# Pooling and projection of an audio layer as one stage, with the row evictions shared between engines

## The reference

```
scores  = sum over features of x * w + b          # per time step
weights = softmax over each window of 8 steps
h       = sum over the window of x * weights      # 94 tokens of 64 features
y       = layernorm(h)
q, k, v = y @ w_qkv.T + b_qkv                     # 8 heads of 8
qgr,kgr = qr(q).Q, qr(k).Q                        # per batch and head
a       = softmax(conv(bn([q.k * s, (q.k)^2 * s, (qgr.kgr)^2 * s])))
h       = h + (a @ v) @ w_proj.T + b_proj
h       = h + ffn(layernorm(h))                   # 16 routed experts and a shared one, 2 layers
```

## Time and profile before

| | |
|---|---|
| median of 3 runs | 902.47 us (901.5 to 903.48) |
| the profiled execution | 902.73 us, its span 900.8 us |
| PE busy | 763.8 us (85%), 16453 instructions |
| PE weight loads busy | 562.5 us (62%) |
| DVE busy | 709.7 us (79%), 1333 instructions |
| ACT busy | 440.2 us (49%), 949 instructions |
| POOL busy | 492.7 us (55%), 532 instructions |
| mean granted TensorE clock | 0.917 |

### The profile page before, as it was taken

How to read it: one execution, slowest core, us unless ns; L and a number is a source line. 1 busy time by engine, 2 the same in 40 slices (tenths; PEclk the granted TensorE clock), 3 DMA queues, 4 the chain that set the end, 5 groups by cost and what they waited for, 6 DMA issues and landing times. The chain is left out here.

```text
span 900.8 us, 38915 instructions
## 1 busy us (share of the span) xinstructions
PE 763.8 (85%) x16453; PEld 562.5 (62%) x16453; DVE 709.7 (79%) x1333; ACT 440.2 (49%) x949; POOL 492.7 (55%) x532
## 2 busy tenths in 40 slices
PE   3577857888616699999999999999999998799994
PEld 2233324666514578777788777788777776366663
DVE  4388895666699489998999998999998998376772
ACT  2234332444302166655556555556655555277773
POOL 3255572000000578888888888888888884122220
PEclk9688886999858599999999999999999999599998
DMA  8766300222410122222222222222222220001111
GB/s 288 279 209 233 107 1 11 43 44 44 105 49 1 60 63 64 62 65 77 65 63 62 64 63 71 71 63 62 62 65 77 66 63 23 1 19 30 30 27 33
DMA packets 65450, 64.99 MB, mean 72 GB/s; under 512 B 39001, under 2 KB 55964, under 8 KB 65308
## 3 DMA queue, kind: packets, MB, share of 16 engines
q1 hardware_dynamic: 64780, 61.24, 22.3%
q10 hardware_dynamic: 528, 1.54, 0.5%
HBM read 52.93 MB, written 6.75 MB: 66 GB/s over the span
## 5 line engine op out<-in xcount | busy, mean ns | idle before, releaser
L1113 ACT ACTIVATE sq<-ps_dot 128x376 f32<-128x376 f32 x384 | 165.0, 482 | 145.7 <-PE ps_dot L1010 145.7
L1010 PE MATMUL ps_dot<-q_st,k_blk 64*64 64x94 f32 x6144 | 170.5, 249 | 1.0 <-ACT sq L1113 0.8
L1010 PEld LDWEIGHTS ps_dot<-q_st,k_blk 64*64 64x64 f32 x6144 | 134.6, 134 | 47.3 <-issue 28.8
L943 POOL TENSOR_TENSOR v_blk<-v_rep,vmask 128x384 f32<-128x384 f32 x128 | 106.7, 855 | 10.6 <-PE ps_m L1040 6.3
L958 POOL TENSOR_TENSOR half<-prob 128x564 f32<-128x564 f32 x64 | 75.6, 1181 | 60.6 <-ACT prob L1108 60.6
L965 POOL TENSOR_TENSOR k_blk<-k_cm,hmask 128x768 f32<-128x768 f32 x64 | 96.7, 1511 | 1.8 <-PE ps_a L1052 1.8
L967 POOL TENSOR_TENSOR k_mix<-k_cm,cols 128x768 f32<-128x768 f32 x64 | 96.8, 1512 | 0.0
L1136 DVE TENSOR_REDUCE row_max<-ps_a 128x94 f32<-128x564 f32 x128 | 88.9, 736 | 5.2 <-PE ps_a L1060 5.2
L357 PE MATMUL ps_spread<-parts,pair_sel 128*128 128x376 bf16 x256 | 57.4, 365 | 34.9 <-DVE prod L467 22.7
L1060 PE MATMUL ps_a<-sq,mix_w 64*32 64x282 f32 x2048 | 82.3, 405 | 0.5 <-ACT sq L1113 0.5
L1105 ACT ACTIVATE prob<-prob,head_const 128x564 f32<-128x564 f32 x64 | 49.1, 767 | 66.2 <-DVE prob L1158 66.2
(11 more groups left out here) (215 smaller groups left out, 1479.1 us busy)
## 6 DMA issues: line engine op xcount, KB each, us to landing
v_rep<-v_rows SPq DMA_DIRECT2D x128, 192.0 KB, 3.1
x_g<-in_x_dram SPq DMA_DIRECT2D x15, 1500.0 KB, 6.6
v_rows<-tok SPq DMA_DIRECT2D x16, 192.0 KB
q_st<-q_cm SPq DMA_DIRECT2D x64, 47.0 KB, 1.9
out_dram<-rows SPq DMA_DIRECT2D x16, 188.0 KB
x_g<-in_x_dram ACTq DMA_DIRECT2D x1, 1500.0 KB, 7.6
top_rows<-tok SPq DMA_DIRECT2D x32, 16.0 KB
top<-top_rows SPq DMA_DIRECT2D x1, 512.0 KB, 3.5
```

Of the source, the lines that this page charges most:

```text
L943: vb = pool.tensor_tensor(v_blk[:, a, b].rearrange("p t (o d) -> p (t o) d", o=H), v_rep[:, a, b].rearrange("p (t o d) -> p (t o) d", o=H, ...
L1010: mm = pe.matmul(ps_dot[64 * v:64 * v + 64, (2 * g + b) % 3, N * c:N * c + N], k_blk[rows, a, SLOTS * (3 * v + g) + c].rearrange("p k h m ...
L1113: act.activation(sq[:, b, :, g, :], ps_dot[:, (2 * g + b) % 3, 0:SLOTS * N].rearrange("p (c n) -> p c n", c=SLOTS), ACT.Square).then_inc(s ...
```

## The change

`pool_windows` and `project` become one stage, `pool_project`, with one loop of 32 steps and four more. A chunk, which is two steps of pairs, starts two steps after its pairs: the pad tokens in step 2c+2, the centring in 2c+3, variance and rows in 2c+4, the grams in 2c+5. The products of pooling are written over x in `x_g`. The weights' four banks and the scores' one leave three banks for the projection: `ps_c` takes the centred tokens, the variances and the grams of a chunk in turn, and `ps_tok` takes its two halves in turn. `sq`, `xc`, `std` and `own` have one buffer.

`EVICT = ("dve", "act")`: the first half's rows are evicted by VectorE as before. The second half's are evicted by ScalarE with a per-partition scale, and GpSimd adds the bias over 96x768 in place. SyncE stores the q and k rows too (384 KB a chunk), to `qk_dram`, and reads them back by group of pairs into `qk_rows`. Queries and keys are turned in `orthogonalise` by matmuls with the identity, chunks 0 to 7 before the experts and 8 to 15 after them. There the square root of the diagonal stands behind the experts' evictions on ScalarE's queue. The bias columns of `ffn_w` are written by ScalarE there, not by VectorE in `constants`.

The core of the new stage, TensorE first:

```diff
+            def centre(c):
+                pe.wait_ge(s["ready"], c + 1)
+                if c:
+                    pe.wait_ge(s["std_done"], c)
+                    pe.wait_ge(s["gram_owned"], c)
+                pe.matmul(ps_c[:, 0:W], k["cent_w"][:], tokens[:, span(c, CP), :].rearrange("p r m -> p (r m)"),
+                          start=True, stop=True).then_inc(s["cent_done"], 1)
+            def variance(c):
+                pe.wait_ge(s["kept"], c + 1)
...
+            def rows(c, h):
+                if h:
+                    pe.wait_ge(drained[0], c + 1)
+                elif c:
+                    pe.wait_ge(drained[1], c)
...
+            def grams(c):
+                for h in range(2):
+                    pe.wait_ge(biased[h], c + 1)
+                pe.wait_ge(s["std_done"], c + 1)
...
+            for i in range(STEPS + 4):
+                if i < STEPS:
+                    spread(i // HP, 2 * (i % HP))
+                c = chunk_at(i, 4)
+                if c is not None:
+                    variance(c)
+                    rows(c, 0)
+                c = chunk_at(i, 5)
+                if c is not None:
+                    grams(c)
+                if i < STEPS:
+                    spread(i // HP, 2 * (i % HP) + 1)
+                c = chunk_at(i, 4)
+                if c is not None:
+                    rows(c, 1)
+                c = chunk_at(i, 3)
+                if c is not None:
+                    centre(c)
```

ScalarE and GpSimd:

```diff
+            def scaled(c, h):
...
+                act.wait_ge(s["tok_done"], 2 * c + h + 1)
+                for e in range(2):
+                    for b in range(2):
+                        r = 2 * h + e
+                        out = act.activation(tok[:, a, r, b, :], ps_tok[:, b, 192 * e:192 * e + 192], ACT.Copy,
+                                             scale=rstd[:, a, 2 * r + b:2 * r + b + 1])
+                out.then_inc(drained[h], 1)
...
+            for i in range(STEPS + 4):
+                c = chunk_at(i, 4)
+                if c is not None:
+                    deviation(c)
+                    if EVICT[0] == "act":
+                        scaled(c, 0)
+                if i < STEPS:
+                    odd_weights(i)
+                if c is not None and EVICT[1] == "act":
+                    scaled(c, 1)
+                c = chunk_at(i, 3)
+                if c is not None:
+                    squares(c)
+                if i < STEPS - HP:
+                    for part in {4: (0, 1), 5: (2,), 6: (3,)}.get(i % HP, ()):
+                        softmax(i // HP + 1, part)
...
+            def bias(c, h):
+                rows = tok[:, c % 2, 2 * h:2 * h + 2].rearrange("p r b f -> p (r b) f")
+                pool.wait_ge(drained[h], c + 1)
+                pool.tensor_tensor(rows, rows, k["bias_row"][:, 0:1, :].broadcast_to([NP, 4, 192]), ALU.add).then_inc(biased[h], 1)
```

VectorE's order in a step:

```diff
+            for i in range(STEPS + 4):
+                if i < STEPS:
+                    product(i)
+                c = chunk_at(i, 4)
+                if c is not None:
+                    inverse(c)
+                    if EVICT[0] == "dve":
+                        rows_out(c, 0)
+                if 1 <= i <= STEPS:
+                    pooled(i - 1, 1)
+                c = chunk_at(i, 5)
+                if c is not None:
+                    gram_own(c)
+                c = chunk_at(i, 2)
+                if c is not None:
+                    pads(c)
+                if i < STEPS:
+                    pooled(i, 0)
+                c = chunk_at(i, 5)
+                if c is not None:
+                    gram_sum(c)
```

ScalarE in `orthogonalise`:

```diff
             act.activation(aug[:, :, :, 2 * D:3 * D], top[:].rearrange("p n k d -> p k d n"), ACT.Copy).then_inc(top_turned, 1)
-            act.wait_ge(dve_step, DIAG_STEP)
-            act.activation(rs[:], diag[:], ACT.Sqrt).then_inc(roots, 1)
+            for l in range(LAYERS):
+                act.activation(k["ffn_w"][:, EXP, l, HID:HID + 1], k["ffn_bias"][:, 32 + l:33 + l], ACT.Copy)
+                act.activation(k["ffn_w"][:, 0:EXP, l, HID], k["ffn_bias"][:, 16 * l:16 * l + 16], ACT.Identity,
+                               bias=k["ffn_bias"][:, 32 + l:33 + l])
+            for c in range(NCH // 2):
+                queries_keys(c, c % 2)
             for n, (l, lo, hi) in enumerate(EXPERT_BANKS):
...
+            act.wait_ge(dve_step, DIAG_STEP)
+            act.activation(rs[:], diag[:], ACT.Sqrt).then_inc(roots, 1)
+            for c in range(NCH // 2, NCH):
+                queries_keys(c, c % 2)
```

More of the change, by code:

```diff
@@ L320, in halves, with chunk_at @@
             return view.rearrange("p (a t) -> p a t", a=2)
+        def chunk_at(i, begun):
+            c, odd = divmod(i - begun, 2)
+            return c if not odd and 0 <= c < NCH else None
         @block.sync
         def _(sp):
-            with sp.Fori(1, NG // 2) as n:
-                for a in range(2):
[L326 to L338, removed]
+            def load(m):
+                g, q = 2 + m // GROUP_LOADS, m % GROUP_LOADS
+                for pooled in (s["even_pooled"], s["odd_pooled"]):
+                    sp.wait_ge(pooled, (g - 2) * HP + 2 * q + 2)
+                load_quarter(sp, x, x_g, x_in, g, g % 2, q)
@@ L340, in _, with score @@
+            for a in range(2):
+                sp.wait_ge(stored[a], 48 * NCH // 2)
         @block.tensor
         def _(pe):
-            def score(a, n, turn):
-                mm = score_pair(pe, x_g, x_in, ps_score, k, a, n, turn)
+            def score(g, n):
+                mm = score_pair(pe, x_g, x_in, ps_score, k, g % 2, n, g // 2)
                 if n == GP - 1:
                     mm.then_inc(s["scores_done"], 1)
[L347 to L362, removed]
@@ L364, in _, with spread @@
-            pe.wait_ge(s["lo_zero"], 1)
-            groups(pe, group)
-        def parted(eng, i, a, part):
+            def spread(g, n):
+                if n == 0:
+                    if g < NG - 1:
+                        pe.wait_ge(s["scores_out"], g + 1)
+                    pe.wait_ge(s["mid_moved"], g + 1)
+                    pe.wait_ge(s["lo_done"], g + 1)
+                pe.wait_ge(s["odd_out" if n % 2 else "even_done"], g * HP + n // 2)
+                for half in range(2):
+                    for part in range(2):
+                        mm = pe.matmul(ps_spread[:, 2 * (n % 2) + half, 0:HALF], k["pair_sel"][:, half, n, :], parts[:, g % 2, part, :],
+                                       start=(part == 0), stop=(part == 1))
+                mm.then_inc(s["spread_done"], 1)
+                if g < NG - 1:
+                    for ahead in AHEAD[n]:
+                        score(g + 1, ahead)
@@ new lines, in centre @@
+            def centre(c):
[7 more added lines that the diff above has]
+                pe.wait_ge(s["kept"], c + 1)
+                for r in range(CP):
+                    mm = pe.matmul(ps_c[0:NP, W + 2 * r:W + 2 * r + 2], sq[:, r, :], k["mean_w"][:, 0:128:64], start=True, stop=True)
+                mm.then_inc(s["var_done"], 1)
@@ L396, in softmax @@
                 if part == 1:
-                    act.wait_ge(s["shifted"], i + 1)
+                    act.wait_ge(s["shifted"], g + 1)
                     act.activation(soft[:], soft[:], ACT.Exp).then_inc(s["exps"], 1)
                 if part == 2:
-                    parted(act, i, a, "hi")
+                    parted(act, g, "hi")
                 if part == 3:
[L402 to L413, removed]
@@ L419, in _ @@
         @block.gpsimd
         def _(pool):
[L421 to L430, removed]
@@ new lines, in gram_own, with gram_sum @@
+            def gram_own(c):
+                dve.wait_ge(s["gram_done"], c + 1)
+                dve.tensor_tensor(own[:], ps_c[:, 0:256].rearrange("p (b g e) -> p b e g", g=4, e=D),
+                                  k["mask4"][:].unsqueeze(1).unsqueeze(1).broadcast_to([128, 2 * CP, D, 4]), ALU.mult).then_inc(s["gram_owned"], 1)
+            def gram_sum(c):
+                dve.wait_ge(s["gram_owned"], c + 1)
+                dve.tensor_reduce(gram[:, span(c, 2 * CP), :], own[:], AX.X, ALU.add)
```

401 lines of the change are left out of this document (191 added, 210 removed).

## The result

The change makes the kernel slower: 931.9 us (median of 4 runs, 929.68 to 936.78) against 901.99 us (4 runs, 900.97 to 903.48), a ratio of 1.034 with a 95% interval of 1.032 to 1.037. The forecast was 920 us, range 894 to 950. The profiled execution took 933.51 us, with a span of 931.5 us.

A forecast was written before the change was run, and what follows sets the result against it. The prediction took one loop of waits through four engines, 10.9 us a chunk, to bound the merged stage. It summed 902.5 + 11.1 (merged stage, clock included) + 6.5 (later root) = 920 us, range 894 to 950.

The forecast's parts named there:

- The loop: Merged stage, grams of one chunk to the next: one chain of waits through four engines, 10.9 us at full clock.
- The start: Merged stage: the first centre can be issued in step 3, at 49.2 us, with nothing before it changed on the path.
- The root: Orthogonalisation: square root of the diagonal starts 6.5 us later, behind the turning of queries and keys; bounds 4 to 12.
- Rival 1: Merged stage: VectorE is the bound because the four-engine loop overlaps better; period 8.4, 868 us; chance 0.16.
- Rival 4: Merged stage: each ScalarE table switch costs about as much again as its load, six times 1.28 us; 928 us; chance 0.05.
- The clock: Merged stage: TensorE's clock falls at the bias wait in about half the periods, 1.5 us each, 12 us together.
- softmax and scores: Merged stage: three softmaxes inside the loop add 3.4 us each, 10.2; scores queued ahead of centre or variance add 3.4.
- My upper bound: Merged stage: a loop all at half clock adds 3.7 us a period, 58 us.
- Rival 3: Merged stage: TensorE stays at half clock for most of it; 966 us; chance 0.10.

The follow-up runs named there:

- e4: The change with the square root of the diagonal taken after the sixth of the ten expert banks, not after the last: 928.0 us.
- e6: The change with grams one step later, behind the odd spread and in the even spread's banks, so the centre no longer waits for them: 878.0 us.
- the run with ten fillers: The change plus ten matmuls with unread results on TensorE just before its wait for the biased rows: 912.2 us.
- e3: The change plus sixteen matmuls (32 instructions) with unread results on TensorE just before its wait for the biased rows: 925.9 us.

## Why the prediction was right in sign and 12 us short

**What held.**
- The loop. All four engines stand on it in the order that was walked, and at full clock it takes 10.86 us against 10.9. The clock falls at the wait for the bias, as was expected: it is 0.88 from 231.20 to 233.88, where TensorE stands, and 0.50 from then on; behind an earlier wait it falls with the grams (0.94 from 181.37 to 182.10, 0.50 from there to 184.80). The two operations that no row showed were bounded well: ScalarE's scaled eviction took 1.34 us (taken: 1.37), the bias 1.80 (taken: 1.65, upper bound 1.8). The extra 0.15 was covered by links of the chain that were 0.05 to 0.2 shorter than walked.
- The start, by luck. The first mask was due at 49.2 - 1.35 + 10.9 + 0.8 = 59.55 and came at 59.57. But the first centre started at 47.49, 1.7 us early, and the mask came 2.33 us behind the first grams (57.24) and not 0.80, because VectorE was still at the first softmax of the loop, which I had counted later.
- The root: 6.2 us later against 6.5, for the reason given; e4 took back 5.4 of it.
- Rival 1 (VectorE is the bound) fell: VectorE is 55% busy and waits 30.6 us for the grams. What it needed is what e6 made: grams that hold up neither the odd spread nor the centre. Then calm periods are 7.7 us, and the time lands at 878, not at the 868 that I gave it.
- Rival 4 (each table load costs again as much) fell. The rule of the Trainium skill, "ScalarE: Activation LUTs", section "What ACT_TABLE_LOAD costs", would have 1.38 us of drain behind a load. The trace doesn't bear it out; here is the load in the softmax of the third group, and the exponential starts 0.02 us after its end:

```profile
109.36 1.28 ACT L483 ACT_TABLE_LOAD   x1
110.66 0.52 ACT L483 ACTIVATE soft<-soft 64x376 f32<-64x376 f32 x1
```

**What failed** is the size of one term, the 12 us of the step "The clock"; its mechanism held. The mean period was 13.57 us, where I had said 10.5 to 12.5. The last mask would have been at 248.65 by my terms (49.2 + 174.4 - 1.35 + 0.8, then 10.2 + 3.4 for softmax and scores, 12 for the clock). It was at 263.20. The difference of 14.55 divides so, by the run with ten fillers. Its fifteen periods sum to 180.5 us, which is 17.6 more than fifteen of 10.86, where I had 13.6 for softmax and scores: 4.0 us of mine were missing (some 2 of them in the last two periods, 12.33 and 11.55 us). These two and the three in which a group begins ran at clocks of 0.63 to 0.87 in that run too and hold 9.3 of the 17.6, so a part of the 4.0 is clock as well; how much, the runs don't separate. The change's fifteen sum to 203.6, so 23.1 are left for its lower clock, where I had 12: 11.1 us were missing. The periods, 10.86 for 10.9, give 0.6 back. As the filler run had 0.91 and not 1.00, 23.1 is if anything too little. The stage was 26.4 us longer and not 11.1; the 0.8 us that 14.55 leaves of this came behind the last mask.

I had both parts of that term too small: that the clock falls in half of the periods, and that a fall costs 1.5 us, because the grams, spread and centre fill TensorE and bring the clock back. In the period at 233.88 it doesn't come back: variance (1.44), both halves' rows (1.60 each) and all between them are at half clock too, and the fall costs 3.4 us. In the calm stretch, from the mask at 182.16 to that at 235.03, no period escapes: they take 12.31, 14.29, 12.46 and 13.81 us at clocks of 0.78, 0.50, 0.77 and 0.62, that is 1.45 to 3.43 us more than 10.86. Against the filler run the first seven periods lose 7.1 us, the last eight 16.0 (the sum of the two, 23.1). That a long period by itself makes the next one slower is not shown: in the calm stretch the four clocks go up and down. The last eight have less for TensorE to do: the scores end in them, and pooling before the last two. My upper bound, 3.7 a period, was of the right size; what I lacked was the weight between the bounds. Rival 3 (half clock throughout, 966 us) was nearer than its 0.10 says, and between it and the forecast lies what happened. I forecast a stage clock of 0.8 to 0.95; it was 0.71.

What brings the clock back after a gap isn't settled by these runs. They show that 1.5 us of extra matmuls in a gap of 2.7 us do as much as 2.4 us.

The gain that the merge seemed to offer went into the one wait that couples the chunks, and into the clock: with the grams out of the loop (e6) 54 us of the 932 are back.

## What to carry to other kernels

When stages are merged, walk the loop through all queues before adding up idle time: here VectorE had 45% to spare, and a queue that stands in front of the grams, with a bank that three products share, made the period. An engine that helps with an eviction lengthens the loop if the next product waits for it (here by 0.47 us a period at full clock), and the longer pause on TensorE can cost more than that through the clock (here 1.45 to 3.43 us a period in the calm stretch). Where such a pause can't be removed, move work of the same queue ahead of the wait (here 17 us), and price half clock at the whole loop's TensorE steps, not at the two behind the pause.

## What the runs showed of the hardware

- A few idle-time matmuls paid for themselves: six a period, whose results nobody reads, made the kernel 19.4 us faster than none, with nothing else changed but the granted clock (0.71 to 0.88; 1.00 in the calm periods).
- Those matmuls (float32, weights of 128x128 loaded for each, 120 columns) took 0.12 us an instruction at full clock (20 in 2.39 us), against 0.042 for the attention's weight loads of 64 columns (24 in 1.01 us). e3 had been planned with 1.7 us for 32, or 0.053 each, and that estimate spoiled it.
- GpSimd's in-place sum over 96x768 took 1.80 us, more than its 128x768 product at 1.51 us: fewer partitions, same elements per partition, and no gain from it. The operands have other forms too, so the runs don't say where the 0.29 us come from.
- ScalarE's eviction with a per-partition scale costs no more than that with a per-partition bias: four of 96x192 in 1.34 us, four of 128x188 in 1.37 us.
